# A sampling loop whose distance and z rows go through PSUM tile by tile, and a further fold on GpSimd for one half

## The reference

```python
offs = conv3x3(gn(x), offset_w, offset_b)          # 9 taps x (y, x)
mask = 2 * sigmoid(conv3x3(gn(x), mod_w, mod_b))   # 9 taps
sy, sx = off_y + row + ky, off_x + col + kx
sampled = bilinear_gather(gn(x), sy, sx) * mask    # 9 taps at every pixel
out = einsum('nckhw,ock->nohw', sampled, weight) + bias
x = x + relu(batch_norm(out))
```

## Time and profile before

| what | value |
|---|---|
| median of three runs | 419.23 us |
| span of the profiled execution, first to last instruction | 422.3 us |
| sampling loop in it, from the taps of pair 0 to the taps of pair 63 | 165.9 to 381.7 us |
| PE, DVE, ACT, POOL busy in the span | 76%, 77%, 59%, 48% |

### The profile page before, as it was taken

One profiled execution on the slowest core, in us unless ns is written; L12 is line 12 of the kernel. 1 busy time (PEld: TensorE's weight loads), 2 busy tenths in 40 slices (PEclk: granted clock), 3 DMA queues, 4 the chain that ended last, 5 costly groups with the idle time before them and its releaser, 6 DMA issues.

```text
span 422.3 us, 14389 instructions
## 1 busy us (share of the span) xinstructions
PE 318.9 (76%) x6057; PEld 207.0 (49%) x6058; DVE 326.1 (77%) x641; ACT 248.1 (59%) x364; POOL 204.2 (48%) x244
## 2 busy tenths in 40 slices
PE   0079999858858409999889989888999889993570
PEld 0022334312213105777767767667777677772460
DVE  5456258833599842999999999989999799997266
ACT  1023323305136205888868888878888688884355
POOL 9770000199491000566654665656666366867000
PEclk9999999969588555999999999999999899997565
DMA  7799200188570634300110101001110000000005
GB/s 224 134 234 232 57 2 0 31 210 246 130 194 5 127 88 102 93 8 28 30 27 3 48 29 28 29 4 47 28 28 8 25 3 3 7 19 2 3 0 199
DMA packets 18106, 28.65 MB, mean 68 GB/s; under 512 B 6890, under 2 KB 7465, under 8 KB 18029
## 3 DMA queue, kind: packets, MB, share of 16 engines
q1 hardware_dynamic: 12397, 19.40, 17.4%
q0 software_dynamic: 2400, 5.07, 5.3%
q10 hardware_dynamic: 3246, 3.27, 3.5%
HBM read 8.03 MB, written 5.83 MB: 33 GB/s over the span
## 4 chain that ended last, share of the span: by engine, by line
PE 43%; ACT 26%; DVE 10%; DMA 7%; SPq 7%; issue 6%; POOL 1%; DVEq 1%; ACTq 1%; POOLq 0%
ACT hx L936 16%; PE ps L645 10%; PE ps L776 9%; ACT zreg L1019 7%; PE ps L588 6%; PE ps L609 5%; PE ps L658 4%; DMA hx<-xpad 3%; SPq L443 3%; PE ps L785 2%; SPq L347 2%; DVE prod L1318 2%; PE ps L599 2%; DMA x_sb<-in_x 1%; DVE x_sb L1413 1%
## 5 line engine op out<-in xcount | busy, mean ns | idle before, releaser
L564 POOL TENSOR_TENSOR prod<-prod 128x416 f32<-128x416 f32 x128 | 134.9, 1076 | 122.2 <-DVE prod L1318 122.2
L1318 DVE TENSOR_TENSOR prod<-ps,hy 128x480 f32<-128x480 f32 (+1 forms) x256 | 137.8, 600 | 14.8 <-PE ps L785 12.2
L785 PE MATMUL ps<-zreg,hx 64*64 64x96 f32 x4608 | 115.5, 250 | 0.0
L936 ACT ACTIVATE hx<-ps 128x576 f32<-128x576 f32 x131 | 78.2, 648 | 49.1 <-PE ps L776 31.6
L785 PEld LDWEIGHTS ps<-zreg,hx 64*64 64x64 f32 x4608 | 103.3, 135 | 7.6 <-issue 0.2
L1023 ACT ACTIVATE hx<-hx,rbias 128x1152 f32<-128x1152 f32 x64 | 81.1, 1267 | 0.0
L1326 DVE TENSOR_REDUCE areg<-prod 128x32 f32<-128x448 f32 x128 | 72.8, 608 | 0.5 <-POOL prod L564 0.4
L645 PE MATMUL ps<-preg,sel 26*128 26x288 bf16 x260 | 43.1, 284 | 31.3 <-ACT zreg L1019 17.8
L776 PE MATMUL ps<-wzp,sreg 128*128 128x144 bf16 x512 | 43.6, 229 | 0.0
L645 PEld LDWEIGHTS ps<-preg,sel 26*128 26x128 bf16 x260 | 20.1, 92 | 47.2 <-issue 29.4
L1019 ACT ACTIVATE zreg<-ps 128x576 f32<-128x576 f32 x64 | 42.1, 658 | 0.0
(11 more groups left out here) (178 smaller groups left out, 359.4 us busy)
## 6 DMA issues: line engine op xcount, KB each, us to landing
scratch<-zreg SPq DMA_DIRECT2D x12, 240.0 KB, 4.3
sreg<-scratch SPq DMA_DIRECT2D x12, 192.0 KB, 2.5
out<-x_sb SPq DMA_DIRECT2D x8, 256.0 KB, 2.1
x_sb<-in_x SPq DMA_DIRECT2D x3, 512.0 KB, 5.0
areg<-xpad POOLq DMA_DIRECT2D x23, 66.0 KB, 3.9
areg<-xpad SPq DMA_DIRECT2D x23, 66.0 KB, 2.9
sreg<-scratch SPq DMA_DIRECT2D x4, 336.0 KB, 3.3
zreg<-xpad POOLq DMA_DIRECT2D x15, 66.0 KB, 4.1
```

The costliest lines, as they stand in the source:

```text
L564: pool.tensor_tensor(slots[:, :, 0:2 * moved], slots[:, :, 0:2 * moved], slots[:, :, 2 * KEPT:6 * KK], ALU.add).then_inc(folded, 1)
L785: return pe.matmul(g_ps(g, h)[u * W:(u + 1) * W, k - TAPS[h][0], :, :], hx[s, (t + u) % 4, k, :], z_sb[s, y + u + k // 3:y + u + k // 3 + ...
L936: act.activation(hx[:, t % 4, :, :].rearrange("p k (h x) -> p h k x", h=2), dist_ps(bank).rearrange("p h (k x) -> p h k x", k=KK), ACT.Abs)\
L1318: mul = vector.tensor_tensor(pv[:, n0:n1], gv, wv[:, n0:n1], ALU.mult)
```

## The change

It does two things. First, in the pair's part on PE the order is distance of tile 0, z rows of tile 0, distance of tile 1, z rows of tile 1, in place of both distances and then both z rows, and each tile has its own waits on its own eviction; ScalarE evicts distance and z rows of tile 0, then of tile 1, each behind its own waits, so that the z eviction of 128x576 becomes two of 128x288. Second, for half g = 0 GpSimd waits for its own fold and folds five more slots (9 to 13 onto 0 to 4, 128x160 elements), so that VectorE's reduction of that half has `KEPT2` = 9 slots, 128x288 elements; half 1 stays at 14. `folded` now counts three a pair.

```diff
@@ gpsimd, behind the fold of half g
+                    if g == 0:
+                        pool.wait_ge(folded, 3 * i + 1)
+                        moved = KEPT - KEPT2
+                        pool.tensor_tensor(slots[:, :, 0:2 * moved], slots[:, :, 0:2 * moved],
+                                           slots[:, :, 2 * KEPT2:2 * KEPT], ALU.add).then_inc(folded, 1)
@@ tensor, ahead of the taps
-                    pe.wait_ge(dist_ready, t + 3)
-                    pe.wait_ge(zrow_saved, t + CREDIT)
                     if y == 0:
                         pe.wait_ge(lead_low, (b + 1) * DVE_LEADS)
                         pe.wait_ge(lead_saved, (b + 1) * (ZLEAD - DVE_LEADS))
                     for u in range(2):
+                        pe.wait_ge(dist_ready, t + u + 2)
+                        pe.wait_ge(zrow_saved, t + u - 1 + CREDIT)
                         distance((t + 2 + u) // HH, (t + 2 + u) % HH, PAIR_BANKS[u])
-
-                    for u in range(2):
                         for h in range(2):
@@ scalar
-                    act.wait_ge(dist_made, t + 4)
-                    act.wait_ge(zrow_made, t + 4)
                     for u in range(2):
+                        act.wait_ge(dist_made, t + u + 3)
+                        act.wait_ge(zrow_made, t + u + 3)
                         distance(t + u + 2, PAIR_BANKS[u])
-                    act.activation(z_sb[:, y + ZLEAD:y + ZLEAD + 2, :].rearrange("p u (h n) -> p u h n", h=2),
-                                   both[:, :, :, KK * HALF:KK * HALF + ZH], ACT.Copy).then_inc(zrow_saved, 2)
+                        act.activation(z_sb[:, y + ZLEAD + u, :].rearrange("p (h n) -> p h n", h=2),
+                                       zt_ps(PAIR_BANKS[u]), ACT.Copy).then_inc(zrow_saved, 1)
@@ vector, add_up
-                vector.wait_ge(folded, 2 * i + g + 1)
+                vector.wait_ge(folded, 3 * i + g + 2)
+                kept = KEPT if g else KEPT2
```

More of the change, by code:

```diff
@@ L39 @@
 KEPT = 14
+KEPT2 = 9
 X_ENDS = (0, 2, 4, 6, 7, 8)
@@ L1009, in _ @@
                         act.wait_ge(xparts_stored, 16 * B * NQ)
-                    both = ps[:, :].rearrange("p (a h n) -> p a h n", h=2, n=BANK)[:, 0:2, :, :]
                     slot = (t + 2) % 4
@@ L1323, in add_up @@
                 b, y = i // (HH // 2), i % (HH // 2)
-                vector.wait_ge(folded, 2 * i + g + 1)
+                vector.wait_ge(folded, 3 * i + g + 2)
+                kept = KEPT if g else KEPT2
                 here = acc[:, y + g * (HH // 2), b, :].rearrange("p (a e) -> p a e", e=2)
                 vector.tensor_reduce(here, prod[:, i % 2 * 2 + g, :]
-                                     .rearrange("p (a n e) -> p a e n", a=C // 2, e=2)[:, :, :, 0:KEPT],
+                                     .rearrange("p (a n e) -> p a e n", a=C // 2, e=2)[:, :, :, 0:kept],
                                      AX.X, ALU.add).then_inc(acc_ready, 1)
```

## The result

The changed kernel takes 418.07 us (median; 415.03 to 419.54), the kernel before 419.96 in the same comparisons. The ratio is 0.993, with a 95% interval of 0.991 to 0.995: 0.7% faster, some 3 us (1.9 us between the medians), where 7.4 us were forecast. By the bound of 1% set ahead it is no change.

A forecast was written before the change was run, and what follows sets the result against it. The prediction took a ring between TensorE and ScalarE as the bound. Saving 58 x (3.25 - 3.09) = 9.3 us, less 1.9 of costs, left 7.4: from 419.23 to 411.8 us, range 406 to 417.5 for 8 in 10.

The forecast's parts named there:

- The ring: Loop: TensorE and ScalarE wait on each other through distances, z rows and their evictions, setting the 3.25 us period.
- The new bound: Loop: with the ring cut, PE's floor of 3.09 us a pair sets the period.
- The loss at two more changes of shape: PE's part of a pair: switching z to distance and distance to z once more adds 0.19 us.
- VectorE's floors of 3.10 and 2.94: VectorE's least time a pair in us: 3.10 without GpSimd's further fold, 2.94 with it.
- the wait in front of tile 1: PE, ahead of tile 1's distance: the new wait is met early and costs nothing.
- A block change itself stays.: Image changes, 6.21 us each: unchanged apart from 0.19 us for the longer distance and z part.
- The sum: Whole kernel: 9.3 us saved over 58 periods, less 1.9 us of costs, leaves 7.4 us.
- one slow pair: Pair behind the last block change: 4.48 us, its taps at about half speed, 1.2 us each time.
- the clock: Rival, block changes: two more half-speed taps add 2.5 us, none saves 1.2; 0.07 together with slower by GpSimd.
- the base of the sum: First profile of the kernel before: span 422.3 us against a median of 419.23, 211.91 us of it between taps.
- the tail: Behind the loop: the last reduction waits for the last fold, so the new fold and its wait add 0.6 us.

The follow-up runs named there:

- e7: Changed kernel with both distances before both z rows and without GpSimd's further fold: 415.88 us, ratio 0.988 to the kernel before.
- e3: Changed kernel with both distances before both z rows, waits and evictions still tile by tile: 405.3 us, ratio 0.966 to the kernel before.
- e2: Changed kernel without GpSimd's further fold, VectorE's reduction keeping 14 slots for both halves: median 420.2 us, ratio 0.990 to the kernel before.
- the second profile: The kernel before, unchanged, profiled once more: 417.76 us, span 416.0.
- e11_fill_second: Changed kernel with only the second idle stretch of PE at a block change filled, by four matmuls behind the sixth lead row: 411.72 us in one execution.

## Why the prediction was wrong, step by step

**Right.** The ring was the bound, and the tile-by-tile order cuts it. The new bound is PE's row of matmuls: period 3.09 forecast, 3.10 measured. The loss at two more changes of shape was put at 0.19; distances and z rows take 2 x 0.70 = 1.40 now, against 1.20 in two groups, and each of four further changes cost 0.10. The Trainium skill's rule that a change of tiling mode drains the TensorEngine (TensorEngine Tiling (Array Packing), Key Properties) agrees with that. Its 128 cycles for a drain (TensorE: Matmul & The Clock Gate, Step-by-step: what each phase is for) make an estimate of 0.05 us a change at 2.4 GHz, half of what the trace and the runs show. VectorE's floors of 3.10 and 2.94 hold (3.11 without the fold in e7, a mean of 2.94 with it in e3), the fold is worth nothing to the period in this change (e2), the new fold takes 0.49 where 0.5 was assumed, and the wait in front of tile 1 costs nothing seen.

**Wrong: "A block change itself stays."** This is the step that failed. The chain through VectorE's copies nearly stayed. From the taps to the next distance the changed kernel takes 215.33 - 210.23 = 5.10 us. The kernel before takes 330.53 - 325.50 = 5.03:

```profile
330.53 0.65 PE L645 MATMUL ps<-preg,sel 26*128 26x288 bf16 x4 [0.59 <-ACT zreg L1004]
```

With the clock held, a block change takes 6.49, 0.27 above the 6.22 before, of which the prediction had 0.19. But PE's clock did not hold. The sum took one slow pair over from the kernel before, at 1.2 us, and the prediction had the clock beyond that as a rival that "widens the range", with two more falls at 1.2 us each. The clock fell at three of three, from the second distance on, at 4.7 us for the three: 3.4 us more than the sum had. The price of 1.2 was read from one pair, in which the fall came only with the taps. With the clock held the changed kernel has a ratio of 0.982, which is the forecast's 411.8 / 419.23. That this agrees so closely is in part luck: the sum kept a slow pair that no longer comes, and had too little for the block changes and the tail.

**Weak: the base of the sum.** The profile of before had a slow pair behind one block change, a slow first pair and a late start. The prediction took the difference to the median as a scale (0.7%) and carried those pairs into the sum as if both kernels shared them. Against the second profile, 213.9 in the loop, the forecast's own terms give 213.9 - 60 x 0.16 + 3 x 0.19 = 204.9, so with the 0.6 of the tail 8.4 us in place of 7.4. With the clock held the loop takes 205.7 (from 163.18 to 368.86 in e11_fill_second), with the clock lost 210.3. That base would have raised the forecast saving by 1 us, farther from what was measured, so the base isn't what made the prediction miss.

**A term of half its size: the tail.** The last reduction ends 0.56 us later behind the last taps (6.62 against 6.06), as the 0.6 had it, and so do PE's first matmuls of the correction (L819, 0.55 later). But PE's matmuls on the rows that GpSimd stages came 10.39 us behind the last taps, and 9.17 in the profile of before: 1.2, not 0.6. The changed kernel:

```profile
379.98 0.62 DVE L1332 TENSOR_REDUCE areg<-prod 128x32 f32<-128x448 f32 x1 [0.57 <-POOL prod L565]
380.14 0.24 POOL L554 COPY wreg<-xpad 128x64 f32 x1 [0.19 <-issue]
380.78 3.44 POOL L554 COPY wreg<-xpad 128x64 f32 x11 [0.40 <-issue]
384.37 2.87 PE L829 MATMUL ps<-zreg,wreg 128*128 x12 [0.69 <-POOL wreg L554]
```

and the kernel before, to be read with the earlier trace rows:

```profile
387.04 3.46 POOL L553 COPY wreg<-xpad 128x64 f32 x12
390.86 2.88 PE L823 MATMUL ps<-zreg,wreg 128*128 x12
```

GpSimd's copies used to start right behind its last fold, in one row; now they stand behind 0.19 and 0.40 us in which the profile shows nothing that GpSimd waited for, and PE waits 0.69 for them. The prediction followed VectorE's branch and left GpSimd's out. The two partial kernels show that the further fold brings this: with the fold alone the same two stretches stand there and the matmuls come 10.39 behind the last taps; with the tile-by-tile part alone the copies stand in one row and they come 9.24 behind. Why the fold opens the two stretches was not tried.

Together, against the second profile of before: 60 x 0.147 = 8.8 saved in the blocks and a stall of 0.3 that didn't recur, less 3 x 0.27 = 0.8 at the block changes, less 4.7 for the clock, less 1.3 in the tail (10.39 against 9.07 in that profile), leaves 2.3 us; the medians differ by 1.9 and the ratio stands for 3. How often the clock falls in the other executions of the kernel before, which have no profile, isn't known.

## What to carry to other kernels

Before a sum is made against one profile, look in it for pairs, rows or stages that differ from their repeats, and take their excess out, or the base is chance. When an order is split to break a ring, count the changes of matmul shape that it adds, and look for a split of waits and evictions that leaves the matmuls grouped: with the fold, that one gained 3.4% here against 0.7%. Where PE idles at a stage's end, price the work behind it at both clocks; a few matmuls that add nothing to the result, placed directly ahead of it, held the clock here.

## What the runs showed of the hardware

A change between matmuls of 26 and of 128 rows cost 0.09 to 0.10 us, taken over both directions (period 3.10 against 2.92 and 3.52), with the new weights loaded only some 0.07 us ahead of the modelled end of the last matmul (290.41 against 290.48). From 128 rows to the 64 x 64 taps it was 0.10, read from one pair of the kernel before and not varied. PE's granted clock went from 2.4 to 1.2 GHz behind idle stretches as short as 0.32 and 0.66 us with 0.78 us of matmuls between them (at three block changes of three), and stayed at 2.4 at three of three when the second was filled although 0.81 us of idle were left. A fold of 160 elements on GpSimd takes 0.49 us, 0.08 more than in proportion to the fold of 416 at 1.07.
